# One weight pass instead of three for the rest chunk of a feed-forward layer, with a new order of the round

## The reference

```
def _layer(x, wqkv, qs, ksc, wo, lg, lb, w1, b1, w2, b2):
    h = shift_token(x)
    q, k, v = jnp.split(h @ wqkv, 3, axis=-1)          # 8 heads of 64
    q, k = rotary_xpos(l2norm(q) * qs, l2norm(k) * ksc)
    o = local_attention(q, k, v)                       # window 128, looks one block back
    x = x + o @ wo
    h = layernorm(shift_token(x)) * lg + lb
    a, g = jnp.split(h @ w1 + b1, 2, axis=-1)          # 2 x 682 columns
    h = a * gelu(g)
    x = x + h @ w2 + b2                                # 682 rows
...
x = x + 0.5 * ffn(layernorm(x))                        # two such layers
x = x + attn(layernorm(x))                             # 16 heads, keys = queries = x, values = the whole x
x = x + 0.5 * ffn(layernorm(x))                        # the same two layers again
```

## Time and profile before

| | us |
|---|---|
| median of 3 runs | 3703.92 (3702.88 to 3707.95) |
| the profiled execution, whole | 3698.05 |
| its span, first to last instruction | 3696.3 |
| TensorE busy | 3455.8 (93%) |
| VectorE busy | 2636.0 (71%) |
| GpSimd busy | 2267.9 (61%) |
| ScalarE busy | 2075.2 (56%) |
| mean granted clock of TensorE | 0.977 of 2.4 GHz |

### The profile page before, as it was taken

The page is one execution under the profiler, slowest core; times in us unless marked ns, Lnnn a source line. Parts: engine busy times, 40 slices in busy tenths (PEclk is TensorE's granted clock), DMA queues, the critical chain, the costliest instruction groups (busy, mean ns, idle before and its releaser), DMA issues.

```text
span 3696.3 us, 69827 instructions
## 1 busy us (share of the span) xinstructions
PE 3455.8 (93%) x21152; PEld 2833.0 (77%) x21152; DVE 2636.0 (71%) x7112; ACT 2075.2 (56%) x4848; POOL 2267.9 (61%) x2307
## 2 busy tenths in 40 slices
PE   4799999899999699999999999997999999899997
PEld 3678777677877588888888888885778777777875
DVE  6687887788888365565555655556787787888884
ACT  2475776577677244444444444444676677567663
POOL 3567667657766355555555555575577666667762
PEclk9799999999999899999999999998999999999999
DMA  4344344434435431212212222203344335434433
GB/s 147 129 151 134 119 150 136 137 110 155 150 119 162 108 70 46 46 50 50 58 47 47 52 56 43 76 24 120 126 135 152 115 131 165 131 120 150 156 115 110
DMA packets 425513, 397.17 MB, mean 107 GB/s; under 512 B 139292, under 2 KB 373416, under 8 KB 425128
## 3 DMA queue, kind: packets, MB, share of 16 engines
q1 hardware_dynamic: 425128, 392.57, 34.5%
HBM read 224.67 MB, written 159.38 MB: 104 GB/s over the span
## 4 chain that ended last, share of the span: by engine, by line
PE 70%; DVE 11%; issue 7%; ACT 7%; POOL 3%; DMA 1%; SPq 1%; DVEq 0%; ACTq 0%; POOLq 0%
PE psum L1475 20%; PE psum L1476 18%; PE psum L1477 18%; PE psum L1611 5%; PE psum L1583 3%; PE psum L1697 3%; ACT probs L938 3%; DVE probs L1181 2%; PE psum L1594 2%; POOL ge_lo L835 1%; DVE ssq L1161 1%; DVE p_blocks L1203 1%; ACT L938 1%; ACT L959 1%; DVE nT_lo L1248 1%
## 5 line engine op out<-in xcount | busy, mean ns | idle before, releaser
L835 POOL TENSOR_TENSOR ge_lo<-ge,ge_hi 128x512 fp32r<-128x512 f32 x512 | 671.2, 1313 | 531.9 <-PE psum L1477 286.4
L796 POOL TENSOR_SCALAR probs<-probs,rz 128x256 f32<-128x256 f32 (+1 forms) x1024 | 447.4, 456 | 507.3 <-DVE rz L1195 507.3
L1011 ACT ACTIVATE ge<-psum 128x512 f32<-128x512 f32 x512 | 306.4, 598 | 671.3 <-PE psum L1697 666.8
L1372 DVE CAST ge_hi<-ge 128x512 fp32r<-128x512 f32 x512 | 268.7, 527 | 505.2 <-ACT ge L1011 502.7
L938 ACT ACTIVATE probs<-probs,nb,rq 128x256 f32<-128x256 f32 (+1 forms) x1024 | 574.9, 564 | 51.0 <-DVE nb L1189 49.8
L771 POOL TENSOR_TENSOR rinv<-ssq,minus_half 128x16 f32<-128x16 f32 x124 | 366.3, 2954 | 27.9 <-DVE ssq L1165 21.1
L1181 DVE CUSTOM_DVE_ANT_0 probs<-psum,mask 128x256 f32<-128x256 f32 (+1 forms) x1024 | 336.3, 383 | 46.9 <-PE psum L1594 35.9
L1475 PE MATMUL psum<-wqkv_hi,hT_hi 128*128 128x512 f32 x768 | 338.0, 440 | 15.2 <-DVE hT_lo L1139 9.1
L1203 DVE STREAM_TRANSPOSE p_blocks<-probs 128x384 f32<-128x384 f32 (+1 forms) x384 | 291.0, 783 | 61.6 <-POOL probs L796 57.8
L1475 PE MATMUL psum<-nT_hi,w_hi 128*128 128x512 f32 x704 | 292.3, 415 | 31.3 <-ACT gate L959 23.7
L1476 PE MATMUL psum<-wqkv_hi,hT_lo 128*128 128x512 f32 x768 | 312.2, 406 | 0.0
(11 more groups left out here) (153 smaller groups left out, 9784.3 us busy)
## 6 DMA issues: line engine op xcount, KB each, us to landing
p_turned<-p_blocks SPq DMA_DIRECT2D x128, 512.0 KB, 2.7
pT<-p_turned SPq DMA_DIRECT2D x512, 128.0 KB, 2.9
p_turned<-p_blocks SPq DMA_DIRECT2D x128, 384.0 KB, 2.6
pT<-p_turned SPq DMA_DIRECT2D x512, 96.0 KB, 2.5
xnext<-stream SPq DMA_DIRECT2D x32, 512.0 KB, 3.8
xmid<-stream SPq DMA_DIRECT2D x32, 512.0 KB, 3.9
gaT<-y_turned SPq DMA_DIRECT2D x256, 64.0 KB, 2.0
y_turned<-probs SPq DMA_DIRECT2D x192, 64.0 KB, 2.9
```

The lines of the kernel that those rows point to most:

```text
L796: last = nc.gpsimd.tensor_scalar(pu, pu, rz[:, h, t:t + 1], 1.0, ALU.mult, ALU.mult)
L835: nc.gpsimd.tensor_tensor(ges[1][:, k % 4, :], ge[:, k % 4, :], f32(ges[0][:, k % 4, :]), ALU.subtract).then_inc(S["g_lo"], 1)
L1011: nc.scalar.activation(ge[:, k % 4, :], RB[k % 2], ACT.Exp, scale=GSCALE, accum_out=gz[:, h, t:t + 1]).then_inc(S["g_exp"], 1)
```

## The change

It does three things.

**1. One pass for w5.** The 128 rows of the last chunk are filled with three sets: rows 0 to 42 hold hi of the hidden values (with the row of ones), rows 43 to 84 the lo halves, rows 85 to 127 hi again. Against them the tile of w2 holds hi, hi and lo. One matmul per 128 tokens then gives the sum of the three passes, so `w5` has 4 matmuls and not 12. Engines can't move data to other partitions in this way, so SP copies them: for the hidden values in two transfers per round (step `hs`, `hid_rest`), for the weights in two transfers per load (step `wr`, `w_rest`). `w5` waits for `hid_in`, which the first pair gives, and not for GpSimd directly. `ul5` and `u5` write 42 and 43 rows, not 128. Two fills of w2 with zeros at the start go.

**2. Weights at first use.** The wait for w1 and w2 moves from the end of the loading round to the first `g` or `a` and the first `w` of the round behind it (`after`). The wait for `bias_ok` stays.

**3. New tables.** The order of the steps and the banks are new for all five engines. No step is dropped but for the above.

```
+REST = (slice(0, HR + 1), slice(HR + 1, 2 * HR + 1), slice(2 * HR + 1, P))
...
-PE_STEPS = ("Q2 v1 v2 S0 K2 Q3 K3 v3 +z0 +z1 S1 -n0 -n1 +k0 +q0 S2 -g0 -a0 -g1 +q1 -a1 S3 S4 -w0 -g2 -g3 S5 S6 "
-            "-a2 -a3 A0 A1 -w1 S7 +k1 -w2 -a4 -g4 A2 A3 -g5 +Q0 +q2 +k2 +Q1 -w3 A4 A5 -w4 -w5 +K0 +q3 W0 W1 B "
-            "A6 A7 +k3 W2 W3 +K1 +v0").split()
+PE_STEPS = ("Q2 v1 S0 Q3 K3 v2 S1 v3 -n0 -n1 +z0 S2 +z1 -a0 S3 -g0 +k0 -g1 -g2 S4 S5 -g3 -a1 -a2 +q0 -a3 A0 A1 "
+            "-w0 S6 S7 +q1 -w1 -g4 A2 A3 -w2 -a4 +K0 -g5 +k1 -w3 +q2 A4 A5 +k2 -w4 -w5 +k3 +q3 W0 A6 A7 W1 B "
+            "+Q0 W2 W3 +Q1 +K1 +K2 +v0").split()
...
+        def hid_rest(m):
+
+            need_apart(sp, (S["pool_u"], (FJ + 1) * (m + 1)))
+            sp.dma_start(f32(hid[0][REST[1], FJ % 2, :]), f32(hid[1][0:HR, FJ % 2, :])).then_inc(S["hid_in"], 16)
+            sp.dma_start(f32(hid[0][REST[2], FJ % 2, :]), f32(hid[0][REST[0], FJ % 2, :])).then_inc(S["hid_in"], 16)
+
+        def w_rest(stage):
+
+            need_apart(sp, (S["w_lo"], w_base(stage) + W_A + W_F))
+            sp.dma_start(f32(w2_s[0][REST[1], FJ, :]), f32(w2_s[0][0:HR, FJ, :])).then_inc(S["w_rest"], 16)
+            sp.dma_start(f32(w2_s[0][REST[2], FJ, :]), f32(w2_s[1][REST[0], FJ, :])).then_inc(S["w_rest"], 16)
...
-        for w_ in w2_s:
-            V.memset(f32(w_[:, FJ, :]), 0.0)
...
-                    pe.wait_ge(S["pool_u"], (FJ + 1) * m + i + 1)
+                    if i < FJ:
+                        pe.wait_ge(S["pool_u"], (FJ + 1) * m + i + 1)
+                    else:
+                        pe.wait_ge(S["hid_in"], 32 * (m + 1))
+                        if after is not None:
+                            pe.wait_ge(S["w_rest"], 32 * (after + 1))
                     for t in range(NT):
+                        if i == FJ:
+                            last = mm(ACC[t // 2][:, (t % 2) * D:(t % 2 + 1) * D], hid[0][:, i % 2, t * P:(t + 1) * P],
+                                      w2_s[0][:, i, :], start=False, stop=True, skip_group_check=True)
+                            continue
...
                 if load is not None:
-                    weights_done(pe, w_base(load) + W_A + W_F)
                     pe.wait_ge(S["bias_ok"], min(load + 1, LAYERS))
```

More of the change, by code:

```diff
@@ L379, in rounds @@
         for j in range(B - 2):
-            a_round(n0 + B + 1 + j, final=B * (call + 1), layer=1)
+            a_round(n0 + B + 1 + j, final=B * (call + 1), layer=1, after=None if j else 2 * call + 1)
         a_round(n0 + ROUNDS - 1, nxt=False, final=B * (call + 1), layer=1)
@@ L627, in first, with a_round @@
                 w_vectors(0)
-            def a_round(n, prev=True, nxt=True, load=None, switch=None, final=0, layer=0, call=call, early=None):
+            def a_round(n, prev=True, nxt=True, load=None, switch=None, final=0, layer=0, call=call, early=None, after=None):
                 if call == 0 and not nxt:
@@ L650, in a_round @@
                         x_ahead(m, 16 * (m + 1 - B) if fresh else None)
+                    if kind == "wr" and after is not None:
+                        w_rest(after)
+                    if kind == "hs":
+                        hid_rest(m)
                     if kind == "keep":
@@ L1549, in some_steps @@
         def some_steps(n, prev, nxt, call, only=None, load=None, switch=None, table=PE_STEPS, part=slice(None),
-                       home=bank, ahead=False):
+                       home=bank, ahead=False, after=None):
             biased = True
-            fresh_qkv, fresh_wo, fresh_w1, fresh_w2 = switch, load if load and load % LAYERS else None, load, load
+            fresh_qkv, fresh_wo, fresh_w1, fresh_w2 = switch, load if load and load % LAYERS else None, after, after
             for kind, i, m in steps(table, n, prev, nxt, only, part):
@@ L1632, in some_steps @@
                     c = "ga".index(kind)
-                    if fresh_w1 is not None and m == n:
+                    if fresh_w1 is not None:
                         weights_done(pe, w_base(fresh_w1) + W_A + KD)
```

64 lines of the change are left out of this document (32 added, 32 removed).

## The result

The changed kernel takes 3812.78 us (median of 4 runs, 3811.22 to 3813.84), the one before beside it 3703.4. The ratio is 1.0302 [1.0289, 1.0315]: slower by 3.0%, where 65 us less were forecast. The profiled execution has a span of 3809.5 us.

A forecast was written before the change was run, and what follows sets the result against it. TensorE, busy 3455.8 of 3696.3 us, was taken as the bound. 30.1 + 27.6 + 9.6 - 2.0 + 0 = 65.3 us less, off the median 3703.92, gave 3638 us; 8-in-10 range 3608 to 3682.

The forecast's parts named there:

- part 1: w5 on TensorE: 4 matmuls per round instead of 12, saving 30.1 us, with the transfers hidden behind other work.
- The cover: TensorE work between w3 and w5, put at 6.1 us, hides hid_hi, hid_lo and the transfer, together 4.4 us.
- Rival D: The w5 transfer hop is on the path, perhaps queuing; slower beyond 8.1 us, 3735 us at 9.1; chance 0.06.
- Eight fewer matmuls at 0.118 us: w5 in each round on TensorE: 0.94 us saved per round, 30.1 us over 32 rounds.
- Part 2: Weights awaited at first use, around the four loading rounds: 17.6 us of waits and 10 of clock, 27.6 us saved.
- Part 3: New step order: 0.3 us saved per round, 9.6 in all, with 2 us lost in the first round.
- Part 4: The two drains: w5's added transfer offset by earlier g4 and hid_hi; 0 us, -1.5 to +1.5 each.
- SP's pT behind the hop: Eight pT transfers behind SP's new wait start up to 3 us later; no cost taken.

The follow-up runs named there:

- experiment 4: The kernel before's tables and banks, with one-pass w5, its 43-row transfer split into 42 and 1, and weights at first use: 3754.91 us, ratio 1.0143.
- experiment 1: The changed kernel with nine SBUF copies of various row counts after its last work, each awaited: 43 rows take 6.30 us, 42 rows 2.48.
- experiment 3: The changed kernel with w5 again as twelve matmuls and no transfers for it: 3617.4 us, ratio 0.9773 to the kernel before.
- experiment 2: The changed kernel with the 43-row transfer of each round issued as 42 rows and 1 row: 3620.76 us, ratio 0.9784 to the kernel before.
- experiments 8 and 9: Changed kernel, 43 rows split into 42 and 1, ScalarE issuing both: 3617.12 us; then also VectorE's F (old-residual subtraction) ten steps earlier: 3605.42 us.
- the best kernel: Changed kernel with split transfer issued by ScalarE, VectorE's F ten steps earlier, and twelve w5 matmuls without transfers in the drains: 3602.88 us, ratio 0.9737.
- experiment 11: The changed kernel with twelve w5 matmuls and no transfers, plus F ten steps earlier on VectorE: 3615.82 us, ratio 0.9774.
- experiment 5: The kernel before with only the feed-forward weight waits moved to the first matmul that reads them: 3669.73 us, ratio 0.9919.
- experiment 6: New order and banks alone, twelve w5 matmuls, no transfers, weight wait still at the loading round's end: 3639.7 us, ratio 0.984 to the kernel before.
- experiment 7: Changed kernel with twelve w5 matmuls, plus three transfers (42, 42, 1 rows) into rows no engine reads, not awaited: 3618.14 us, ratio 0.9777.

## Why the prediction was wrong

**The step that failed** is in part 1: "I take 2.5 us from the end of hid_lo to the data, with 2.0 and 3.5 as bounds". Measured are 8.7 us in an ordinary round (423.61 to 432.32) and, with nothing else in the queue, still 6.35 from the issue. With the 43 rows cut in two the hop takes 3.7 us from the end of hid_lo (experiment 4), so 5.0 us are the count of rows, and even the rest is over the upper bound of 3.5. The neighbours in the earlier trace rows were chosen by bytes, 64 and 128 KB. The difference lay in plain sight in the diff, as `REST[2]`: 43 rows. None of those rows shows a transfer of a prime number of rows, and a fixed time plus bytes does not describe one: 48 rows, which are more bytes than 43, took 2.29 us (experiment 1).

"The trace of before has no such transfer" was wrong as well. The step `shift` copies from SBUF to SBUF on SP's queue, in three transfers, and VectorE's wait in the earlier trace rows is for them. Two of the three issues in the trace of before, ahead of the statistics at 370.05:

```profile
366.00 0.67 SPq L560 DMA_DIRECT2D nrm<-xmid  x1
366.71 0.91 SPq L561 DMA_DIRECT2D nrm<-xmid  x1
```

From the first issue to the data are 4.05 us, in the next round 3.42 (435.08 to 438.50), and one issue takes 0.7 to 0.9 us, not the 0.4 that I took. These rows would have given the good hop. And L560 moves 112 rows and L561 the 15 that are left (`SHIFTED = P - 16`): the kernel before doesn't move its 127 rows in one transfer.

**The cover was right.** I put 6.1 us from w3's end to w5. In the trace w3 ends at 421.54 and w4 at 427.62, 6.1 us. w5 starts 10.8 us behind w3's end, so 4.7 were open, and the row says 4.70.

**Rival D was the case**, as to the place and what waits for what. The reason that it gave, a hop that queues behind other transfers, was not what made the hop slow. Its chance was set at 0.06 from the same 2.5 us. Its price, the round grows by the excess, was too low: 4.7 x 32 - 65 is +85, measured is +109. Beside experiment 3, which has the same order and first use and no pack, the profiled execution is 190 us longer: 169 are waits for the hop, 61 are the same matmuls at a lower clock (experiment 2), 26 come off for the pack's fewer matmuls, and the remaining 15 off is other idle time that got shorter. The clock stood nowhere in D's price. What it set against the waits, 65, was too small, since order and first use alone give 83; without that the result would be worse still.

**Eight fewer matmuls at 0.118 us**: right. The ordinary round of the first layer with the pack and a good hop is 66.98 us, without the pack 67.92, 0.94 apart, as forecast. But the sum of 32 such rounds, 30.1, was too much: 13 us are left in the best kernel. "All of this is on the path" was said of TensorE's waits as they were, and not of what waits next when w5 ends 0.9 us sooner. In 14 rounds of the second layer F on VectorE took the gain (experiments 8 and 9), in the rounds before the drains the hop isn't covered, and the rest goes at the seams (experiment 11), where it was counted but not explained.

**Part 2**: right. 27.6 us forecast, 30.6 measured alone (experiment 5). The rounds behind a load came out at 70.3 to 73.7 us in that run, forecast 71 to 74. In the changed kernel they are at 75 to 76, with the hop's wait in them.

**Part 3**: mis-sized. 9.6 - 2.0 = 7.6 us forecast, 60.7 measured alone (experiment 6). Two steps of it: the wait of Q3 and K3 for GpSimd was put at 1.05 us a round and is 0.3, so an ordinary round gains 1.1 us and not 0.3. And I looked at ordinary rounds alone, while 38 us of the gain lie elsewhere: in the loading, switching and following rounds, and around the attention. What in the order shortens these was not taken apart.

**Part 4**: wrong. A drain's hop costs: w5 waits 8.1 us in each. With the 43 rows cut in two it still waits 4.5 and 4.4 (the run of experiment 2).

**SP's pT behind the hop**: I took nothing for it, and that is right (experiment 7). In the changed kernel too TensorE's waits for pT are 10.4 us in all, against 15.4 before.
